# Delta memory: six values at a group's end, mixing quarters built by halves, a routing step moved

## The chip, the cores and the metric

The kernel runs on one core of one Trainium2 chip. Its engines are TensorE (PE; PEld is its weight load), VectorE (DVE), ScalarE (ACT), GpSimd (POOL) and SyncE (SP). The metric is the device time of one execution in microseconds, the median of several runs.

## The reference, cut to what matters

The whole is linear attention, a mixture-of-experts layer (top 2 of 8 experts), a fast-weight ("delta") memory with layer norm, and the expert layer again, each added to x. The change lies in the delta memory and its seam with the second routing. The memory works on 512 batches of 8 steps, 16 heads of 64 values:

```
k = k / sum(k); q = q / sum(q)            # k, q are elu(.) + 1
denom_acc = cumsum(k); key_denom = <shifted denom_acc, k>   # 1 at the first step
beta = sigmoid(beta) * key_denom; k = k / (key_denom + EPS)
for t in range(8):                        # per batch and head, W starts at 0
    delta = beta_t * (v_t - W k_t)
    W = W + outer(delta, k_t)
    out_t = W q_t
layer_out = SCALE * out / (<denom_acc, q> + EPS)
x = x + layer_norm(h + layer_out @ w_o.T) # then the router of the second expert layer
```

## The kernel before, in words

`delta_memory` splits the 512 batches into four groups of 128 (NG = 4), each of 1024 tokens. The kernel never keeps W: for each group it computes all products of keys with keys and queries within a batch ("gram"), solves an 8-step triangular system per batch and head for mixing coefficients, and multiplies the values by these. The stages of group g, or of m = g - 1 where the work is one group behind:

- *Values.* `values(m)` on TensorE (L1839 is `project_value`) makes 16 tiles of 128x512, each of four instructions in the stream (two passes, each with its weight load). ScalarE copies each to `v` (L2023). For m < 3 only the first 12 are made here (LATE_VALUES), with `turn(m + 1)`, the transposes of the next group's h (L1834), ahead of value 8.
- *Keys and queries of g.* For each of eight head pairs TensorE makes four projections (L1897) into a ring of four PSUM banks, ScalarE takes an exponent (L2060), VectorE combines the two into `kq` (L2327) and frees the bank. Then TensorE makes the pair's 128 small products (L1919), and ScalarE copies the two banks out (`gram_copy`, L2049 and L2052). VectorE puts the steps of the former group's solve between its tiles (BESIDE). Values 14 and 15 of m come before the last pair's products, 12 and 13 after them.
- *Store, load, solve.* The products go to DRAM by eight DMAs each from SyncE and GpSimd and come back by one (`load_coef`, L1638). `solve(m, i)`, i = 0 to 16, is a chain of small VectorE instructions from L2176 (betas), L2182 (`key_sums`, which waits for the load) to L2242 (`scale_out`). SyncE then stores and loads the coefficients again (L1646, L1654) as `mix_tok`.
- *Mixing of m.* For each pair p TensorE multiplies values by a spread form of the coefficients (L1967, 64 matmuls in two halves of a bank pair), ScalarE copies the result (L2094), and one pair later TensorE projects it out (`project_out`, L1950). The spread form is made in quarters of the heads: 0 and 1 by VectorE (`build`, L2253), 2 and 3 by ScalarE (its own `build`, L2082, eight instructions of one step each), after the pairs p = 1 and p = 3, needed at p = 4 and p = 6.

The order on each engine is written out by hand, in one function body per engine; each engine runs its instructions in that order and waits for counting semaphores.

Between these stages lie the steps of the second expert layer's router, in eight rounds r of 512 tokens. A round is: normalise (VectorE), `turn` (TensorE transposes, L241), copy (ScalarE, L262), `score` (L247), `choose` (VectorE, from L187), `rank` (TensorE, L254) and the exponent (ScalarE, L266), `place` (VectorE: `weigh` from L210 and `placed` up to L233), then `send`, eight indirect DMAs from GpSimd (L277). All rounds share one PSUM bank, `b_r`. The semaphore `place_ready` is raised once by `begin` and once by each `place`; `turn` waits for it:

```
    def turn(self, pe, r):
        pe.wait_ge(self.place_ready, r + 1)
```

In `mix_values(m)` for m = 1 and 2 TensorE does round 2m - 2 at p = 0, 1, 2 (turn, score, rank) and turn and score of round 2m - 1 at p = 5 and 6; its rank comes in the next `values`. VectorE's steps between the groups are the list of calls near L2440.

## Time and profile before

| | us |
|---|---|
| median of 3 runs | 982.95 (982.76 to 984.05) |
| the profiled execution's own time | 982.38 |
| its span, first to last instruction | 980.7 |
| TensorE busy | 926.1 |
| VectorE busy | 553.3 |
| ScalarE busy | 541.6 |
| GpSimd busy | 370.3 |

The profile is of one execution. Its rows give times from the span's start, so a position such as 562.6 can be found in the timeline of every engine. Matmuls overlap, and a stretch of matmuls ends somewhat before the sum of start and duration says; the distance between two starts is the safer measure. "Idle before" is how long an engine stood before a row, and the name behind the arrow is the instruction that seems to have released it; "issue" means that the profile shows nothing it waited for.

### The profile page before, as it was taken

The numbers are of one execution on the slowest core, as the hardware profiler recorded it, in microseconds if no ns is written. First come the engines' busy times: TensorE is split into PE (matmuls) and PEld (weight loads), VectorE is DVE, ScalarE is ACT, GpSimd is POOL, SyncE is SP. The second block draws the span as 40 slices with busy tenths as digits, with TensorE's granted clock in tenths as the row PEclk, the third lists the DMA queues.
The fourth block names the chain that finished last, engine by engine and source line by source line (L and its number), as shares of the span: only waits on it lengthen the run. The fifth ranks groups of instructions, "written<-read, shape, count | busy, mean of one in ns | idle before, by whom it ended". The sixth has DMA issues, their size and how long they took to land.

```text
span 980.7 us, 31631 instructions
## 1 busy us (share of the span) xinstructions
PE 926.1 (94%) x11919; PEld 689.4 (70%) x11919; DVE 553.3 (56%) x1966; ACT 541.6 (55%) x1082; POOL 370.3 (38%) x387
## 2 busy tenths in 40 slices
PE   7999999999999999987999899999998999989994
PEld 6446655665679999984554485568456779988994
DVE  5236465355376542206679658777885887774114
ACT  3543243334314555544776675785677585666772
POOL 2300412321333776653141012122531264866773
PEclk9999999999999999998999999999999999999998
DMA  8744224404403233205020120111024513123346
GB/s 220 231 89 88 63 53 105 108 15 97 110 23 75 78 97 99 69 24 173 3 88 4 46 89 1 47 49 53 24 58 135 171 48 77 59 72 99 94 123 220
DMA packets 80308, 82.77 MB, mean 84 GB/s; under 512 B 12207, under 2 KB 63236, under 8 KB 79648
## 3 DMA queue, kind: packets, MB, share of 16 engines
q1 hardware_dynamic: 66240, 59.61, 23.0%
q0 software_dynamic: 10176, 19.04, 6.1%
q10 hardware_dynamic: 3744, 2.10, 0.9%
q8 instruction: 99, 1.62, 0.7%
q14 instruction: 49, 0.40, 0.1%
HBM read 53.96 MB, written 27.64 MB: 83 GB/s over the span
## 4 chain that ended last, share of the span: by engine, by line
PE 38%; DVE 8%; ACT 4%; issue 3%; DMA 1%; POOL 0%; DVEq 0%; ACTq 0%; POOLq 0%; SPq 0%
PE b_ring L1897 8%; PE b_ring L1348 6%; PE b_ring L1359 6%; PE b_ring L1839 5%; PE b_g L1950 4%; PE b_g L1919 4%; PE b_ring L1967 2%; ACT early L2082 2%; DVE b_kq L2327 2%; ACT b_outT L2094 1%; DVE b_coef L2238 1%; PE b_r L247 1%; PE b_s L1906 1%; DVE b_prod L2235 0%; PE b_g L1339 0%
## 5 line engine op out<-in xcount | busy, mean ns | idle before, releaser
L1897 PE MATMUL b_ring<-b_hT,b_qkT 128*128 128x512 f32 x256 | 120.9, 609 | 5.9 <-DVE b_kq L2327 4.6
L2327 DVE SCALAR_TENSOR_TENSOR b_kq<-b_exp,b_ring 128x512 f32<-128x512 f32 x128 | 83.0, 684 | 32.1 <-ACT b_exp L2060 30.4
L277 POOL DMA_INDIRECT expert_rows<-f_route_sent,f_route_place_id x64 | 62.4, 976 | 97.5 <-DVE f_route_place_id L233 50.9
L2060 ACT ACTIVATE b_exp<-b_ring 128x512 f32<-128x512 f32 x128 | 73.6, 604 | 30.5 <-PE b_ring L1897 18.0
L1897 PEld LDWEIGHTS b_ring<-b_hT,b_qkT 128*128 128x128 f32 x256 | 45.1, 189 | 62.4 <-issue 39.8
L1021 ACT ACTIVATE phik<-a_ring 128x512 f32<-128x512 f32 x64 | 38.2, 597 | 81.4 <-PE a_ring L864 81.4
L277 POOL DMA_INDIRECT expert_rows<-g_route_sent,g_route_place_id x48 | 53.2, 1108 | 76.8 <-PE b_ring L1967 31.1
L1348 PE MATMUL b_ring<-b_v,b_kq 128*128 128x128 f32 x568 | 76.1, 278 | 3.1 <-issue 2.8
L1359 PE MATMUL b_ring<-wide,b_v 128*128 x568 | 75.9, 277 | 0.6 <-ACT b_v L1389 0.4
L1348 PE MATMUL a_ring<-phik 128*128 128x128 f32 x568 | 75.0, 275 | 0.4 <-ACT phik L1369 0.4
L1359 PE MATMUL a_wide<-wide,phiqT 128*128 x568 | 74.7, 275 | 0.0
L1321 POOL DMA_INDIRECT expert_parts<-phiqT,a_rn_wide x59 | 59.2, 1004 | 39.7 <-ACT phiqT L1389 14.9
L1348 PEld LDWEIGHTS b_ring<-b_v,b_kq 128*128 128x128 f32 x568 | 70.1, 194 | 3.7 <-issue 3.2
L1359 PEld LDWEIGHTS b_ring<-wide,b_v 128*128 128x128 f32 x568 | 69.8, 194 | 1.0 <-issue 1.0
L1348 PEld LDWEIGHTS a_ring<-phik 128*128 128x128 f32 x568 | 69.1, 192 | 0.7 <-issue 0.7
L1359 PEld LDWEIGHTS a_wide<-wide,phiqT 128*128 128x128 f32 x568 | 69.0, 192 | 0.0
L1950 PE MATMUL b_g<-b_oT,b_outT 128*128 128x128 f32 x512 | 64.9, 281 | 4.0 <-ACT b_outT L2094 3.9
L1383 DVE COPY phik<-wide 128x512 f32 x71 | 30.6, 437 | 66.8 <-PE a_ring L1348 59.8
L1321 POOL DMA_INDIRECT expert_parts<-b_v,b_hT x56 | 57.0, 1018 | 23.1 <-PE b_ring L1348 10.9
L1950 PEld LDWEIGHTS b_g<-b_oT,b_outT 128*128 128x128 f32 x512 | 59.4, 191 | 6.4 <-ACT b_outT L2094 4.1
L864 PE MATMUL a_ring<-feat_k,a_xnT 128*128 128x512 f32 x128 | 60.8, 610 | 0.8 <-ACT a_xnT L1015 0.8
L1374 ACT ACTIVATE phiqT<-a_ring 128x512 f32<-128x512 f32 x71 | 42.4, 597 | 34.5 <-PE a_ring L1348 34.5
(340 smaller groups left out, 1845.3 us busy)
## 6 DMA issues: line engine op xcount, KB each, us to landing
a_rn_wide<-norm_compact SPq DMA_DIRECT2D x28, 512.0 KB, 8.4
wide<-in_L_ffn_W SPq DMA_DIRECT2D x32, 256.0 KB, 5.2
a_rn_wide<-expert_rows SPq DMA_DIRECT2D x71, 65.0 KB
b_coef<-gram_compact SPq DMA_DIRECT2D x4, 1024.0 KB, 5.0
b_hT<-expert_rows SPq DMA_DIRECT2D x56, 65.0 KB
x<-in_L_attn_a_x SPq DMA_DIRECT2D x8, 256.0 KB, 4.5
early<-expert_parts SPq DMA_DIRECT2D x4, 512.0 KB, 5.7
gram_compact<-wide SPq DMA_DIRECT2D x32, 64.0 KB
```

The costliest lines, as they stand in the source:

```text
L277: pool.indirect_dma_start(self.rows, bass.IndirectOffsetOnAxis(self.place_id[:, k, n:n + 1], 0), self.sent[:, n, k, :], None).then_inc(sel ...
L864: ins = pe.matmul(bank[:, :], xnT[par][:, n * P:(n + 1) * P], A["feat_k"][:, half * 512:half * 512 + 512], start=True, stop=True)
L1321: pool.indirect_dma_start(self.parts, bass.IndirectOffsetOnAxis(self.blk[u][:, DIM + 1:ROW].bitcast(U32), 0), self.y[u], None, bounds_chec ...
L1348: ins = pe.matmul(self.hid_bank[j % 2][:, f * P:(f + 1) * P], self.w1_now[:, b % W1_SLOTS, f * P:(f + 1) * P], self.blkT[:, b % HID_SLOTS, ...
L1359: ins = pe.matmul(self.y_bank[j % 2][:, 0:P], self.hidT[:, b % HID_SLOTS, f, :], self.C["w2"][:, bass.ds(e, 1), f, :].rearrange("p a c -> ...
L1374: act.activation(self.hidT[:, b % HID_SLOTS, :, :], self.hid_bank[j % 2][:, :].rearrange("p (f n) -> p f n", f=FC), ACT.Relu).then_inc(sel ...
L1839: pe.matmul(value_bank(k)[:, :], hT[:, m % 2, (k // 2) * P:(k // 2 + 1) * P], C["b_vT"][:, (k % 2) * 512:(k % 2) * 512 + 512], start=True, ...
L1897: pe.matmul(ring[n % 4][:, :], w, hT[:, g % 2, half * 512:half * 512 + 512], start=True, stop=True)\
L1919: ins = pe.matmul(g_bank[hh][32 * j:32 * j + 32, a * 64:(a + 1) * 64], kq[r, p % 2, 4 * a + j, 0:T * FOUR], kq[r, p % 2, 4 * a + j, KEYS + ...
L1950: ins = pe.matmul(g_bank[t // 4][:, (t % 4) * P:(t % 4 + 1) * P], outT[:, p % 2, t, :, :], C["b_oT"][:, p, :], start=(p == 0 and t % 4 == ...
L2060: act.activation(exps[:, n % EXPS, :], ring[n % 4][:, :], ACT.Exp, bias=-1.0).then_inc(S["exp_ready"], 1)
L2327: dve.scalar_tensor_tensor(out=kq[:, p % 2, half:half + FOURS // 2, slot:slot + T * FOUR], in0=exps[:, n % EXPS, :].rearrange("p (a n) -> ...
```

## The change

It has five parts. For m = 0 to 2 six values come late instead of four: 14 and 15 before the last pair's products as before, 12 and 13 in the middle of them, 10 and 11 after them. The PSUM banks of the mixing are turned by two, and each wait is set to the new order. ScalarE's quarters are built in two halves of four instructions, after the pairs 1, 2, 3 and 4 instead of whole ones after 1 and 3. In VectorE's list before the last mixing `build(3, 1)` comes directly behind `build(3, 0)`, ahead of `place(3)`. And `place(2)` comes behind the whole of `solve(3, ...)` instead of before it. The arithmetic is the same.

```diff
--- before.py
+++ after.py
@@ -1584,8 +1584,10 @@
 
             return late_res if m == 2 else res
 
-        LATE_VALUES, FIRST_VALUES = 12, 2
-        BESIDE_VALUES, AFTER_VALUES = (14, 15), (12, 13)
+        LATE_VALUES, FIRST_VALUES = 10, 2
+        BESIDE_VALUES, WITHIN_VALUES, AFTER_VALUES = (14, 15), (12, 13), (10, 11)
+
+        LAST_BLOCK = AFTER_VALUES[0] // 2
 
         def values_beside(g):
 
@@ -1593,7 +1595,7 @@
 
         def nth_value(m, k):
 
-            return k if m == NG - 1 or k < LATE_VALUES else (BESIDE_VALUES + AFTER_VALUES).index(k) + LATE_VALUES
+            return k if m == NG - 1 or k < LATE_VALUES else (BESIDE_VALUES + WITHIN_VALUES + AFTER_VALUES).index(k) + LATE_VALUES
 
         def values_between(m):
 
@@ -1890,8 +1892,8 @@
                         n = 4 * p + k
                         if n >= 4:
                             pe.wait_ge(S["kq_ready"], 32 * g + n - 3)
-                        elif g > 0 and n < 2:
-                            pe.wait_ge(S["v_ready"], 16 * (g - 1) + LATE_VALUES - 1 + n)
+                        elif g > 0 and n >= 2:
+                            pe.wait_ge(S["v_ready"], 16 * (g - 1) + LATE_VALUES - 3 + n)
                         kind, half = k // 2, k % 2
                         w = C["b_qkT"][:, (1 - kind) * HD + p * P:(1 - kind) * HD + (p + 1) * P]
                         pe.matmul(ring[n % 4][:, :], w, hT[:, g % 2, half * 512:half * 512 + 512], start=True, stop=True)\
@@ -1913,6 +1915,10 @@
                         pe.wait_ge(S["att_read"], g - 1)
                     wait_apart(pe, S["kq_ready"], 32 * g + 4 * p + 4, K.passed)
                     for a in range(NTAU):
+                        if g > 0 and p == PAIRS - 1 and a == NTAU // 2:
+                            pe.wait_ge(S["kq_ready"], 32 * g + 32)
+                            for k in WITHIN_VALUES:
+                                project_value(g - 1, k)
                         for j in range(4):
                             for hh in range(2):
                                 r = slice(hh * DH, (hh + 1) * DH)
@@ -1929,7 +1935,7 @@
                         spare_values(g)
                     products(p)
                 if g > 0:
-                    pe.wait_ge(S["kq_ready"], 32 * g + 32)
+                    pe.wait_ge(S["v_ready"], 16 * (g - 1) + LATE_VALUES + len(BESIDE_VALUES))
                     for k in AFTER_VALUES:
                         project_value(g - 1, k)
 
@@ -1957,18 +1963,18 @@
                         pe.wait_ge(S["spread_built" if p < 4 else "late_built"], 2 * m + p // 2 % 2 + 1)
                     if p >= 2:
                         pe.wait_ge(S["outT_ready"], 16 * m + 2 * p - 2)
-                    for a in (*range(NTAU - 2), NTAU - 1, NTAU - 2):
-                        if p == 0 and a == NTAU - 2:
+                    for a in (*range(LAST_BLOCK), *range(NTAU - 1, LAST_BLOCK - 1, -1)):
+                        if p == 0 and a == LAST_BLOCK:
                             pe.wait_ge(S["v_ready"], 16 * (m + 1))
                         for j in range(2):
                             r = slice(j * DH, (j + 1) * DH)
                             for hh in range(2):
                                 hd = (2 * p + hh) * DH
-                                ins = pe.matmul(ring[(2 * p + j) % 4][hh * DH:(hh + 1) * DH, :]
+                                ins = pe.matmul(ring[(2 * p + j + 2) % 4][hh * DH:(hh + 1) * DH, :]
                                                 .rearrange("c (t a b) -> c t a b", t=T, a=NTAU)[:, :, a, :],
                                                 v[r, a, hd:hd + DH], spread[r, p // 2 % 2, (2 * p + hh) % QH, a, :, :],
                                                 start=True, stop=True)
-                            if a == NTAU - 2:
+                            if a == LAST_BLOCK:
                                 ins.then_inc(S["mixed_full"], 1)
                     if p >= 1:
                         project_out(p - 1)
@@ -2064,7 +2070,7 @@
                     act.wait_ge(S["own_step"], 2)
                     act.wait_ge(S["parts_added"], 6)
                 m, beside = values_beside(g)
-                for k in beside:
+                for k in (*beside, *(WITHIN_VALUES if g > 0 else ())):
                     copy_value(m, k)
                 gram_copy(PAIRS - 1)
                 for k in AFTER_VALUES if g > 0 else ():
@@ -2072,16 +2078,17 @@
                 act.wait_ge(S["beta_logit"], g + 1)
                 act.activation(beta[:, 0:T, :], sums[:, 0:T, 0:HEADS], ACT.Exp, scale=-1.0).then_inc(S["beta_exp"], 1)
 
-            def build(m, q):
+            def build(m, q, half):
 
                 n = 4 * m + q
                 act.wait_ge(S["tok_loaded"], 32 * (m + 1))
                 act.wait_ge(S["mixed_full"], 4 * (n - 1))
                 by_head = mix_tok[:, :, :, :].rearrange("p a t h -> p h (a t)")[:, q * QH:(q + 1) * QH, :]
-                for b in range(T):
+                for b in range(half * T // 2, (half + 1) * T // 2):
                     ins = act.activation(spread[:, q % 2, :, :, :, :].rearrange("p h a t b -> p h (a t) b")[:, :, :, b], by_head,
                                          ACT.Copy, scale=own[:, b:b + 1])
-                ins.then_inc(S["late_built"], 1)
+                if half:
+                    ins.then_inc(S["late_built"], 1)
 
             def mix_values(m):
                 for n in range(16):
@@ -2091,9 +2098,9 @@
                         act.wait_ge(S["att_done"], PAIRS * m + p - 1)
                     if n == 0 and 0 < m < NG - 1:
                         act.wait_ge(S["x_ready"], m)
-                    act.copy(outT[:, p % 2, :, j, :], ring[n % 4][:, :].rearrange("c (t b) -> c t b", t=T)).then_inc(S["outT_ready"], 1)
-                    if j == 1 and p in (1, 3):
-                        build(m, 2 + p // 2)
+                    act.copy(outT[:, p % 2, :, j, :], ring[(n + 2) % 4][:, :].rearrange("c (t b) -> c t b", t=T)).then_inc(S["outT_ready"], 1)
+                    if j == 1 and 1 <= p < 5:
+                        build(m, 2 + (p - 1) // 2, (p - 1) % 2)
                     if j == 1 and m == NG - 1:
                         if p in (4, 6):
                             routing(routes_of_mixing(m)[0], (p - 4) // 2)
@@ -2439,15 +2446,15 @@
 
             solve(3, 0)
             choose(2)
-            place(2)
             for i in range(1, SOLVE_PARTS):
                 solve(3, i)
+            place(2)
             choose(3)
             residual(2)
             output_statistics(2)
             build(3, 0)
+            build(3, 1)
             place(3)
-            build(3, 1)
             output_normalize(2)
             for i in range(2):
                 scale_and_add(dve, 2, i)
```

## Rows read from the trace of the kernel before

**Rows 1.** the page's part 1: busy us of each engine (share)

```profile
PE 926.1 (94%) x11919; PEld 689.4 (70%) x11919; DVE 553.3 (56%) x1966; ACT 541.6 (55%) x1082; POOL 370.3 (38%) x387
```

**Rows 2.** TensorE's waits over the span: who for whom, us in total, times, longest

```profile
PE b_g L1919 <- issue: 5.2, 2, 2.7
...
PE b_ring L1897 <- DVE b_kq L2327: 4.6, 8, 1.5
PE b_g L1950 <- ACT b_outT L2094: 3.9, 6, 1.0
```

**Rows 3.** TensorE's timeline, group 1's end: start, us, what, [idle before <-releaser]

```profile
562.62 0.31 PE L1919 MATMUL b_g<-b_kq 64*32 64x64 f32 x1 [2.56 <-issue]
562.86 3.54 PE L1839 MATMUL b_ring<-b_vT,b_hT 128*128 128x512 f32 x4
```

**Rows 4.** the timeline of all engines, group 2's end

```profile
650.32 1.98 PE L1839 MATMUL b_ring<-b_vT,b_hT 128*128 128x512 f32 x4
...
652.24 1.66 PE L1967 MATMUL b_ring<-early,b_v 64*64 64x64 f32 x64
```

**Rows 5.** the timeline of all engines, group 3's end

```profile
742.50 0.43 PE L1919 MATMUL b_g<-b_kq 64*32 64x64 f32 x24 [2.69 <-issue]
...
742.86 3.17 PE L1839 MATMUL b_ring<-b_vT,b_hT 128*128 128x512 f32 x4
```

**Rows 6.** windows: us, busy PE, PEld, DVE, ACT, POOL, granted clock, DMA

```profile
562.50:566.50 4.00, 3.88 (x14) 1.47 (x18) 3.29 (x4) 2.58 (x4) 0.85 (x2) 0.57 0.03 8
...
440.00:450.00 10.00, 4.69 (x22) 4.72 (x23) 4.03 (x13) 2.50 (x5) 2.91 (x2) 0.50 0.66 208
```

**Rows 7.** keys of groups 1 to 3: a window, then TensorE's and VectorE's timelines

```profile
511.00:544.00 33.00, 29.69 (x596) 14.06 (x592) 30.91 (x66) 20.55 (x32) 7.84 (x7) 1.00 0.10 35
...
607.56 1.29 DVE L2327 SCALAR_TENSOR_TENSOR b_kq<-b_exp,b_ring 128x512 f32<-128x512 f32 x2
...
608.30 1.99 PE L1897 MATMUL b_ring<-b_hT,b_qkT 128*128 128x512 f32 x4 [0.42 <-DVE b_kq L2327]
...
695.17 0.69 DVE L2327 SCALAR_TENSOR_TENSOR b_kq<-b_exp,b_ring 128x512 f32<-128x512 f32 x1 [1.08 <-ACT b_exp L2060]
```

**Rows 8.** the timeline of the mixings of m = 0 and m = 1

```profile
569.44 5.17 ACT L2082 ACTIVATE early<-b_mix_tok,b_own 128x256 f32<-128x256 f32 x8
...
575.57 2.05 PE L1950 MATMUL b_g<-b_oT,b_outT 128*128 128x128 f32 x16 [0.64 <-ACT b_outT L2094]
...
670.04 2.05 PE L1950 MATMUL b_g<-b_oT,b_outT 128*128 128x128 f32 x16 [1.01 <-ACT b_outT L2094]
```

**Rows 9.** timelines of all engines: load of coefficients, place, solve, turn

```profile
572.97 0.34 SPq L1638 DMA_DIRECT2D b_coef<-gram_compact  x1
...
578.05 0.25 DVE L2182 RECIPROCAL b_rsum<-b_coef 128x16 f32<-128x16 f32 x1 [9.36 <-DMA b_coef<-gram_compact]
...
752.58 0.33 SPq L1638 DMA_DIRECT2D b_coef<-gram_compact  x1
...
756.43 0.17 DVE L210 TENSOR_SCALAR g_route_denom<-g_route_ratio 128x4 f32<-128x4 f32 x1 [1.94 <-ACT g_route_ratio L266]
...
759.12 0.17 DVE L233 CAST g_route_place_id<-g_route_place_of 128x8 uint32<-128x8 f32 x1
...
759.20 0.25 DVE L2182 RECIPROCAL b_rsum<-b_coef 128x16 f32<-128x16 f32 x1
...
765.47 0.47 PEld L241 LDWEIGHTS b_r<-ident,g_route_sent 128*128 128x128 f32 x4
...
776.28 1.22 DVE L2242 SCALAR_TENSOR_TENSOR b_mix<-b_mix,b_rden 128x1024 f32<-128x1024 f32 x1
```

**Rows 10.** the timeline of the last mixing

```profile
789.45 2.10 PE L1967 MATMUL b_ring<-early,b_v 64*64 64x64 f32 x128 [0.36 <-ACT b_v L2023]
...
792.25 2.29 DVE L2253 TENSOR_TENSOR early<-b_mix_tok,b_own 128x2048 f32<-128x2048 f32 x1
...
794.60 1.16 PE L1967 MATMUL b_ring<-early,b_v 64*64 64x64 f32 x64 [0.73 <-DVE early L2253]
```

## The prediction

> **What bounds the kernel now.** I read the page's busy times first: TensorE is busy for 94% of the span, no other engine for more than 56% [rows 1]. So a change pays only where it takes idle time out of TensorE, and costs what idle time it puts in. Next I read the list of waits for TensorE alone [rows 2]. Three kinds stand out, all in the memory part: 5.2 us in two stops within the head products (L1919), put down to "issue"; 3.9 us in six waits of the output projection (L1950) for ScalarE's copies; 4.6 us in eight waits of the key projections (L1897) for VectorE. Then I read the timeline around each group's end, since all edits lie there.
>
> At the end of group 1 TensorE stops for 2.56 us one matmul short of the end, then the two late values take 3.54 us [rows 3]. Group 3 does the same: 2.69 us, then 3.17 us [rows 5]. Group 2 has no stop, and its two values take 1.98 us [rows 4]. The granted clock over 562.5 to 566.5 is 0.57 [rows 6]: the stop also drops the clock to 1.2 GHz for a while. That such a stop is TensorE running out of fetched instructions is my reading, not shown.
>
> **The change, part by part.** Working time is the profiled run's: 982.38 us, span 980.7; the median of three is 982.95, 0.57 more.
>
> *Values.* Per group m = 0 to 2 values 10 and 11 leave the stage before the keys and come after the last products; 12 and 13 come amid these. Nothing is added on TensorE: four passes take 1.9 us wherever they stand (650.32 to 652.24 in [rows 4]). What matters is who limits the stretch they leave. In group 1's keys, VectorE is busy 30.9 of 33 us [rows 7], and TensorE waits for it up to 543 us: the 1.9 us freed before become a longer wait, gain 0. In group 2 VectorE reaches its first key at 607.56 and TensorE waits again at 608.30 [rows 7]: gain 0. In group 3 VectorE idled 1.08 us before its first key [rows 7]: gain 1.1 of the 1.9. The bounds are 0 and 1.9 each; I take these.
>
> At the other end the two values amid the products cost 1.9 us before the products finish. In groups 1 and 3 they run while TensorE would otherwise stop, if the fetch comes as late after it was asked for as before: products finish at 562.9 and with no net cost. Bounds: the whole stop moves elsewhere (+1.9) to both vanish (-0.8). Group 2 has no stop to fill: +1.9. The values after the products in group 1 then run at 2.4 GHz: 3.54 - 1.98 = -1.6. The first mixing pair must end with the block that needs them; ScalarE copies the products first, so the first 64 mixing matmuls take 0.5 more, as in group 2 today (1.66 for 1.16) [rows 4]: -1.1 in group 1.
>
> By the Trainium skill (TensorE: Matmul & The Clock Gate, "HAM oscillation — how this bites in real kernels") time spent throttled costs half of itself. The trace agrees: 3.54 for 1.98. The same section warns only of idle gaps longer than either stop here, by which the values behind them would run at full clock; the rows show otherwise, and they decide.
>
> *Quarters by halves.* ScalarE builds eight parts of a quarter in 5.17 us at a stretch, and TensorE waits 0.64 after each in m = 0 and 1.01 once in m = 1 and in m = 2 [rows 8]. In halves ScalarE spends 2.6 + 1.1 (two copies) per pair against TensorE's 3.1 (1.1 mixing, 2.0 projection): it falls back 0.6 per pair over four pairs but starts a pair ahead, and by my count each copy is just in time. Gain 1.2 in m = 0, 1.0 in m = 1 (bounds 0 and all of it). The new order of PSUM banks only follows the values; the waits keep their distance. 0.
>
> *Builds of the last group together.* VectorE's second build today starts at 792.25, after place(3), and TensorE waits 0.73 for it [rows 10]. Both at once: -0.7; place(3) comes 2.3 later but its consumers (GpSimd's sends) have their own pace. Bounds -0.7 and +0.5 (a later root on GpSimd).
>
> *place(2) behind the whole of solve(3).* This is the edit that decides. It frees VectorE to start solve(3) when its coefficients land: asked for at 752.58, and 5.1 us later by the same load in m = 0 (572.97 to 578.05), so at 757.7 instead of 759.20 [rows 9]. That is worth at most 1.5 us on the way to the last mixing, where TensorE's values end just beside the build: I take 0.4. But place(2) ends with the increment of place_ready, and Router.turn (L238) waits on TensorE for place_ready >= r + 1. For r = 3 that is 4: one from begin, one each from place(0), place(1), place(2). The turn of route 3 stands in mix_values(2) at p = 5, at 765.47 [rows 9], and the diff leaves it there. Behind it in TensorE's queue are the rest of that mixing, all 16 values of the last group and its mixing. So TensorE will stand at that turn until place(2) is done.
>
> When is that? solve(3) takes 759.20 to 777.50 (776.28 + 1.22), 18.3 us of back-to-back VectorE work; place takes from 756.43 to 759.29, 2.9 [rows 9]. Start 757.7 + 18.3 + 2.9 + 0.1 = 779.0, against 765.5: +13.5, if nothing before moved. Bounds of this term: +13.4 with the page's median of 5.0 us to land, +15.0 if the coefficients land only at 759.2.
>
> This time hangs on the end of group 3's products (store, load, solve), so gains up to there count and gains between there and the turn do not. Up to there: -1.1 (group 1), -1.2 (m = 0 halves), +1.9 (group 2), -1.0 (m = 1 halves), -1.1 (keys 3), 0 (group 3, 1.9 against its stop) = -2.5. The turn comes at 776.5, +11.0. The gains of m = 2 (full clock for its values, its halves) only make TensorE arrive earlier, near 761, and wait some 15 us.
>
> After a stop the clock falls: +1.6, the excess of the values behind a stop of 2.56 [rows 3]. From 440 to 450 it stood at 0.50 throughout [rows 6], with TensorE busy for under half of that; half of these 10 us bounds it at +5. From the turn TensorE has the same 24.0 us of work to the last mixing (765.47 to 789.45 [rows 9, 10]), less 0.4 where it waited for VectorE. In the last mixing -0.7, and -0.2, the rest of L1950's 3.9 us. VectorE, GpSimd and the expert stage follow TensorE as today, since they too wait for its values and mixings.
>
> Sum: +11.0 + 1.6 - 0.4 - 0.9 = +11.3, so 993.7 on the profiled run's scale and 994.0 with half of the 0.57 to the median.
>
> **Rivals.**
> (1) Stall as told, but the gains ahead of it don't come: fetch stops move with the matmuls, and halves let ScalarE fall behind. For: the stops depend on positions in the instruction stream, which this shifts by eight. Against: the waits for copies are plainly the 5 us builds. +13.5 + 1.6 + 0 = 997.5. A longer low clock gives the same size.
> (2) The stall is short: TensorE's turn isn't held by place(2), or solve(3) is far shorter with VectorE undisturbed. Then the gains decide: -2.5, another 1.2 at the clock and 1.0 from the halves of m = 2, 0.9 in the last mixing: 982.4 - 5.6 = 976.8, faster. It decides once place(2) is done before about 761. Against: the count of the semaphore is in the code, and the solve's steps depend on each other; I find no way.
> (3) The change of order costs about what the rest gains: a stop of 5 to 6 us, 982 to 983. It would need two thirds of the solve gone.
>
> **How the numbers follow.** Forecast 0.83, rival 1 0.11, rival 2 0.04, rival 3 0.02. The forecast's terms run from 990 (all gains at their best bound) to about 996.5 (clock low for longer); with rival 1, 8 in 10 lie in 990 to 998. A measurement of this kernel tells 0.2% (2 us) from no change: faster 0.04, same 0.02, slower 0.94.
>
> **What would show it.** In the profile after: TensorE's L241 in the third mixing waiting 13 to 17 us for VectorE's place_id (L233), with nothing on TensorE meanwhile, and the granted clock at half behind it; VectorE's L2182 of m = 3 released by the DMA; no L1950 wait for b_outT above 0.3 us; stops in the last products of groups 1 and 3 under 1 us, and L1839 behind them at 2.0, not 3.5 us. TensorE's waits for b_kq in groups 1 and 2 grow by up to 1.9 us each. Wrong would be a third mixing that runs through, or one where another wait than the turn holds TensorE.

## The result, and the profile after

The changed kernel is slower: median 999.71 us of five runs (998.80 to 1000.33), beside 982.76 us for the kernel before in five runs (979.66 to 984.05). The ratio is 1.0185, 95% interval 1.0169 to 1.0200. Forecast were 994.0 us and a range of 990 to 998, so the sign and the mechanism came out and the size did not: the measured median lies 1.7 us above the range. The profiled execution took 998.8 us, span 997.1, where before it took 982.38 us, span 980.7.

Line numbers moved by 2 to 7: head products L1919 are now L1925, keys L1897 are L1899, output projection L1950 is L1956, values L1839 are L1841, mixing L1967 is L1973, the solve's first line L2182 is L2189, GpSimd's shift L1724 is L1726.

The page's part 1 (busy us by engine) of the kernel after:

```profile
PE 929.6 (93%) x11919; PEld 692.2 (69%) x11919; DVE 555.1 (56%) x1966; ACT 540.7 (54%) x1082; POOL 368.4 (37%) x387
```

Counts are those of [rows 1]: the work is the same, and TensorE's share fell because the span grew. The list of waits for TensorE alone says why. Here it is for the kernel after (who for whom, us in total, times, longest):

```profile
PE b_r L241 <- DVE g_route_place_id L233: 17.4, 1, 17.4
PE b_ring L1899 <- DVE b_kq L2334: 9.1, 9, 2.2
...
PE b_g L1925 <- issue: 1.2, 3, 0.6
...
PE b_g L1956 <- ACT b_outT L2101: 0.6, 2, 0.3
```

Against [rows 2]: one new wait of 17.4 us; the waits for VectorE in the keys went from 4.6 to 9.1; the two long stops (5.2) and the waits for ScalarE's copies (3.9) are nearly gone. All four movements were named in the forecast; the first two are larger than it had them.

The new wait, in the timeline of all engines of the kernel after: the coefficients' load, what VectorE does with them, and the turn on TensorE.

```profile
752.57 0.33 SPq L1640 DMA_DIRECT2D b_coef<-gram_compact  x1
...
759.58 0.25 DVE L2189 RECIPROCAL b_rsum<-b_coef 128x16 f32<-128x16 f32 x1 [6.41 <-DMA b_coef<-gram_compact]
...
776.65 1.23 DVE L2249 SCALAR_TENSOR_TENSOR b_mix<-b_mix,b_rden 128x1024 f32<-128x1024 f32 x1
...
780.47 0.17 DVE L233 CAST g_route_place_id<-g_route_place_of 128x8 uint32<-128x8 f32 x1
...
780.70 1.12 PE L241 MATMUL b_r<-ident,g_route_sent 128*128 128x128 f32 x4 [17.36 <-DVE g_route_place_id L233]
```

Compare [rows 9]. VectorE now stands idle for 6.41 us until the coefficients land. Before, place(2) (2.9 us) lay in that gap and cost nearly nothing: the coefficients landed 6.4 us after 752.58, at 759.0, and the solve began at 759.20. Now it lies behind 18.3 us of solve, and TensorE, which has finished its third mixing as far as the turn, waits for it.

What that does to the clock, in windows (us, busy PE, PEld, DVE, ACT, POOL, granted clock, DMA) of the kernel after:

```profile
562.50:566.50 4.00, 4.00 (x125) 2.37 (x124) 2.71 (x4) 3.36 (x6) 0.10 (x1) 1.00 0.02 4
...
768.50:780.50 12.00, 0.00 (x0) 0.00 (x0) 10.79 (x39) 0.00 (x0) 0.00 (x0) 0.51 0.17 51
780.50:785.70 5.20, 5.00 (x77) 4.56 (x78) 0.14 (x1) 1.66 (x3) 2.07 (x2) 0.50 0.58 146
785.70:790.00 4.30, 4.30 (x94) 4.21 (x93) 1.92 (x18) 1.07 (x2) 0.00 (x0) 1.00 0.28 65
```

The first window was at 0.57 before [rows 6] and is at full clock now: the stop at group 1's end is gone. But the long stop puts TensorE at 1.2 GHz (0.51), and it stays there (0.50) for 5 us after it has resumed.

**Where the 16.4 us came from.** I cut both profiled executions at the same instructions (start of the first turn-transpose of the memory part, start of each group's last head product, start of solve(3), of the turn of route 3, of the last mixing, of the expert stage) and compare the stretches. The last column splits the forecast's sum in the same way:

```
us                              before   after   diff   forecast
up to the memory part            452.9   453.6   +0.7    0
group 0, to its last product      47.8    48.4   +0.6    0
groups 1 to 3, to last product   242.0   240.7   -1.3   -2.5
last product to solve(3)          16.5    16.9   +0.4   -1.5
solve(3) to turn of route 3        6.4    21.1  +14.7  +14.9
turn to last mixing               23.8    26.2   +2.4   +1.2
last mixing to expert stage       28.3    27.0   -1.3   -0.9
expert stage to end              162.9   163.1   +0.2    0
sum                                             +16.4  +11.2
```

### The profile page after: what moved, and what is told of

It is laid out like the page before. It is cut to its first block, busy times and chain, and to the rows that moved or that the text cites. A ratio compares the mean times of both kernels' runs of the same rounds, so it can differ in the third digit from the quotient of the medians.

```text
span 997.1 us, 31639 instructions
## 1 busy us (share of the span) xinstructions
PE 929.6 (93%) x11919; PEld 692.2 (69%) x11919; DVE 555.1 (56%) x1966; ACT 540.7 (54%) x1082; POOL 368.4 (37%) x387
## 4 chain that ended last, share of the span: by engine, by line
PE 35%; DVE 14%; issue 2%; DMA 1%; ACT 1%; SPq 0%; DVEq 0%; POOL 0%; ACTq 0%; POOLq 0%
PE b_ring L1899 7%; PE b_ring L1348 6%; PE b_g L1956 5%; PE b_ring L1359 5%; PE b_g L1925 4%; PE b_ring L1841 3%; PE b_ring L1973 3%; DVE b_kq L2334 2%; DVE b_coef L2245 1%; DVE b_h L111 1%; DVE b_prod L2242 1%; DVE b_outT L111 1%; DMA b_coef<-gram_compact 1%; DVE b_ln_stats L90 0%; PE b_s L1908 0%
## 5 line engine op out<-in xcount | busy, mean ns | idle before, releaser
L1899 PE MATMUL b_ring<-b_hT,b_qkT 128*128 128x512 f32 x256 | 122.7, 617 | 10.3 <-DVE b_kq L2334 9.1
L1899 PEld LDWEIGHTS b_ring<-b_hT,b_qkT 128*128 128x128 f32 x256 | 45.7, 191 | 68.2 <-issue 39.8
L1956 PE MATMUL b_g<-b_oT,b_outT 128*128 128x128 f32 x512 | 65.7, 283 | 0.6 <-ACT b_outT L2101 0.6
L1956 PEld LDWEIGHTS b_g<-b_oT,b_outT 128*128 128x128 f32 x512 | 60.3, 194 | 2.7 <-issue 0.8
```

Of the source, the lines that this page charges most:

```text
L1899: pe.matmul(ring[n % 4][:, :], w, hT[:, g % 2, half * 512:half * 512 + 512], start=True, stop=True)\
L1956: ins = pe.matmul(g_bank[t // 4][:, (t % 4) * P:(t % 4 + 1) * P], outT[:, p % 2, t, :, :], C["b_oT"][:, p, :], start=(p == 0 and t % 4 == ...
```

## The experiments

Chips differ. e1 to e4, e6 to e8 and b1 ran on one chip, c0, e5, b2 and b3 on a second, and c1, e9 and e10 on a third. On the first two the stages outside the memory part take some 50 to 65 us longer in every kernel, the one before included (medians of 1037 to 1047 us, against 978.9 on the third). So each kernel is judged by its ratio to the kernel before on the same chip, and a percentage of 1040 is a little more us than one of 980.

### Is it the place? One line each way

Theory: the wait at the turn is the whole loss. Rival: the other edits cost, and the wait only shows where the time is lost.

**e1**, the changed kernel with place(2) back:

```
             choose(2)
+            place(2)
             for i in range(1, SOLVE_PARTS):
                 solve(3, i)
-            place(2)
             choose(3)
```

> The changed kernel with place(2) put back ahead of solve(3, 1); all else stays changed. Theory (TensorE stands at the turn of round 3 until place(2) raises place_ready): L241's wait of 17.4 us goes. TensorE's values of the last group then end near 786.5 on the changed kernel's scale, but the last builds wait for coefficients that go by load (759.6), solve (18.3), store and load (9.4) and one build (2.3), about 789.7 against 806.9 now: 17 us less, so 982 to 983, no gain over the kernel before. Rival (TensorE is held there by something else, such as the late sends or ScalarE's halves): stays above 990. Rival of the prediction (the other edits gain 5.6): 977.

Measured 1.0004 (0.9973 to 1.0034): the loss is gone. The wait for place_id is absent from TensorE's list. A gain of 5.6 us from the other four parts together, as in the prediction's rival 2, would be 0.9946, outside the interval.

**e2**, the kernel before with only place(2) moved behind the solve:

> The kernel before with only place(2) moved behind solve(3). Theory: the whole loss is in this edit. With coefficients landing at about 759.5 the turn comes near 780.5 instead of 765.5, plus about 2.5 for the low clock behind the stop, less 0.4 later: +17, about 999.5. As the prediction had it (landing 5.1 us after issue, low clock worth 1.6): +14.7, about 997.5. Rival (the loss is shared with the other edits): below 993.

Measured 1.0151 (1.0108 to 1.0195): the loss is there without any other edit. From TensorE's list of waits in this kernel:

```profile
PE b_r L241 <- DVE g_route_place_id L233: 14.0, 1, 14.0
```

**e8**, the changed kernel with place(2) amid the solve:

```
             for i in range(1, SOLVE_PARTS):
                 solve(3, i)
+                if i == 5:
+                    place(2)
-            place(2)
```

> The changed kernel with place(2) after solve(3, 5) instead of after the whole solve. Theory: place(2) ends near 759.6 + 8.4 + 2.8 = 770.8 on the changed kernel's scale, so TensorE waits 7.6 us at the turn instead of 17.4, and comes to the last mixing 9.9 us sooner: 989 to 990. The loss is linear in the time of place(2), until it ends before about 763. Rival (it is the sum of VectorE's work, not the place of this step): 999.7.

Measured 1.0087 (1.0059 to 1.0116). Its timeline: the solve's start, the place, the turn.

```profile
784.15 0.25 DVE L2189 RECIPROCAL b_rsum<-b_coef 128x16 f32<-128x16 f32 x1 [5.62 <-DMA b_coef<-gram_compact]
...
795.28 0.17 DVE L233 CAST g_route_place_id<-g_route_place_of 128x8 uint32<-128x8 f32 x1
...
795.50 1.12 PE L241 MATMUL b_r<-ident,g_route_sent 128*128 128x128 f32 x4 [6.80 <-DVE g_route_place_id L233]
```

From the solve's start to the turn it is 11.4 us here, 21.1 behind the whole solve (21.1 in e2, e6, e7, e9 and both profiles of the changed kernel alike) and 4.9 with the place ahead of it (e1). From group 3's last product to the last mixing it is 46.1 us ahead and 53.6 midway; behind it is 61.3 and 61.8 in e7 and e6 on the same chip, and 64.2 and 63.0 in the two traces of the changed kernel. The time follows the position of that one call. One position between the ends was measured, so that the loss is linear is not shown.

### The other edits, one at a time

**e3**, only the values (place, halves and builds as before):

> The kernel before with only the new order of the values and the turned banks. Theory: the gain at the group ends (two stops of 2.6 us filled, full clock behind them) is given back, since group 2 has no stop, groups 1 and 2 wait for VectorE anyway, and in group 3 GpSimd's shift(3) starts 1.7 us sooner and falls on VectorE's output_normalize(1), which takes 5.0 instead of 2.1 us and stops TensorE 2.2 us: 983, within 1.5 of before. Prediction's view (no collision): 980 or less.

Measured 1.0030 (0.9999 to 1.0061): no gain; a loss is not clear of the noise.

**e4**, only the quarters by halves:

```
-            def build(m, q):
+            def build(m, q, half):
...
-                for b in range(T):
+                for b in range(half * T // 2, (half + 1) * T // 2):
...
-                    if j == 1 and p in (1, 3):
-                        build(m, 2 + p // 2)
+                    if j == 1 and 1 <= p < 5:
+                        build(m, 2 + (p - 1) // 2, (p - 1) % 2)
```

> The kernel before with only ScalarE's quarters built by halves. Theory: the waits of L1950 for b_outT (3.9 us) fall to under 1; -3 us if the last mixing's start follows TensorE, -2.3 if it stays with the coefficients' chain: 979.5 to 980.5. Rival (ScalarE falls behind): 983 or more.

Measured 0.9976 (0.9951 to 1.0000), a gain at the edge of what these runs resolve. Its list of TensorE's waits has the copies' wait at the size of the full change:

```profile
PE b_g L1950 <- ACT b_outT L2095: 0.6, 2, 0.3
```

It was 3.8 us in six waits in c0, the kernel before profiled once more (below). But from group 3's last product to the last mixing it takes 46.1 us, only 0.6 less than before (46.7 in both traces): the coefficients' chain (store, load, solve) sets the end there. e4's trace also lacks the stop before group 3's last products (2.69 us before, 2.42 in c0). The stop is missing in e10 and b2 too, which leave the values as they were, so it comes and goes with other edits, and how much of e4's gain is the copies' and how much this stop's isn't separated.

**e5**, only the last group's two builds together:

> The kernel before with only the last group's two builds together. Theory: TensorE's 0.73 us wait for the second build goes, and router waits behind it: -0.7 to -1.3 us, ratio 0.999. Rival (place(3) later delays GpSimd's sends and a root behind them): 1.0005 or more.

Measured 1.0001 (0.9973 to 1.0028), with the kernel before profiled once more beside it (c0, 1047.78 us):

> The kernel before itself, for a trace on the chip of the experiments, where all kernels take some 5% longer. If that is the chip's DMA (the two attention and expert parts), the stretch from the end of group 0's products to the end of group 3's is 242 us as on the first chip and the one from there to the last mixing 46.7, within 1; if the chip is slower altogether, both are longer in proportion.

The stretch from the last mixing to the expert stage is 31.2 us against 32.7 in c0, where the clock was also low for 3.4 us of it. The run as a whole doesn't show it: 1.5 us are 0.14% and below what these runs resolve. As to c0's own question, the stretch from group 0's products to group 3's is 243.5 us (242.0 on the first chip) and from there to the last mixing 46.7 (46.7). The first is half a us beyond the "within 1" that was expected; in proportion to the whole it would be 258. So the extra time of this chip lies outside the memory part.

### What made it 5 us worse than forecast?

Two things in the trace of the changed kernel were not in the sum. First, a GpSimd instruction (shift(3)) ran into VectorE's output_normalize(1), which then took longer. Timeline of all engines of the kernel after, keys of group 3:

```profile
690.69 5.00 DVE L111 TENSOR_SCALAR b_outT<-b_outT,b_ln_out_meanvar,b_ln_out_rstd 128x128 f32<-128x128 f32 x8
...
692.98 2.36 POOL L1726 TENSOR_TENSOR x<-x,ln_b 128x1024 f32<-128x1024 f32 x1
...
696.34 5.40 PE L1899 MATMUL b_ring<-b_hT,b_qkT 128*128 128x512 f32 x8 [2.24 <-DVE b_kq L2334]
```

Before, shift(3) started at 694.71, behind output_normalize(1), and this took 2.14 us:

```profile
691.96 2.14 DVE L111 TENSOR_SCALAR b_outT<-b_outT,b_ln_out_meanvar,b_ln_out_rstd 128x128 f32<-128x128 f32 x8
...
694.71 2.37 POOL L1724 TENSOR_TENSOR x<-x,ln_b 128x1024 f32<-128x1024 f32 x1
```

GpSimd's rows go out once LATE_VALUES values are in, now 10 rather than 12, so all its work behind them starts sooner. Second, the coefficients took 7.0 us to land (752.57 to 759.58), not 5.1. Right behind them SyncE asks for the expert weights, in this kernel as in the one before.

**e6**, the changed kernel, shift(3) held until output_normalize(1) is done:

```
                 pool.wait_ge(S["h_ready"], m + 2)
+                if m in (3,):
+                    wait_apart(pool, S["normed"], m - 1, K.passed)
                 pool.tensor_tensor(x_group(m)
```

> The changed kernel with GpSimd's shift(3) held until output_normalize(1) is done. Theory (the two instructions hold each other up): VectorE's L111 of b_outT near 690 goes from 5.0 back to 2.1 us, TensorE's wait for b_kq there from 2.24 to under 1, the clock doesn't fall at 697, and all later work comes about 3 us sooner: 996.5. Rival (VectorE is late for its own order of work): unchanged, 999.7.

Measured 1.0155 (1.0122 to 1.0187). Its timeline has VectorE back at its old pace, and the shift behind it:

```profile
711.38 2.30 DVE L111 TENSOR_SCALAR b_outT<-b_outT,b_ln_out_meanvar,b_ln_out_rstd 128x128 f32<-128x128 f32 x8
...
713.85 2.36 POOL L1728 TENSOR_TENSOR x<-x,ln_b 128x1024 f32<-128x1024 f32 x1 [0.20 <-issue]
```

So the collision is what stretches VectorE's row. Group 3, from group 2's last product to its own, took 92.6 us against 94.3 and 94.4 in the two kernels on the same chip that kept the collision (e7, e8). The ratio lies between what was expected of the theory (1.014) and of the rival (1.017) and decides nothing.

**e7**, the changed kernel, expert weights asked for only when the last coefficients are in:

```
+            wait_apart(sp, S["coef_loaded"], NG * 16, K.passed)
             load_experts(sp, C, inp, C["w_in"][1])
             store_mix(NG - 1)
```

> The changed kernel with SyncE's loads of the expert weights held until the last coefficients have landed. Theory (the 1 MB of coefficients took 7.0 us instead of 5.1 since the weights' loads share the DMA engines): they land 5.1 us after issue, the turn comes 1.9 us sooner, 997.8. Rival (the load is as slow alone): unchanged, 999.7.

Measured 1.0180 (1.0150 to 1.0210): no gain, as the rival had it.

**b1**, e1 with shift(2) and shift(3) held as in e6:

> The changed kernel with place(2) back and GpSimd's shift(2) and shift(3) each held until the output_normalize beside it is done. Theory: 3 us from shift(3); shift(2) fell on a substitution step of VectorE (2.57 instead of 0.43 us near 603) in both kernels, up to 2 us more, if it does not hold up the next steps instead: 977.5 to 980. Rival (the collision only moves on to the following steps of VectorE): 981 to 983.

Measured 1.0012 (0.9980 to 1.0044): no gain over e1 (1.0004), where 977.5 to 980 us (about 0.995 to 0.997) were expected.

On the third chip the question was whether collision and load together are the missing 5 us. c1 is the changed kernel once more, **e9** is e6 and e7 together:

> The changed kernel itself, beside the experiments. By the parts: place(2) alone 1.015, the rest 1.0004, so 1.0155 to 1.018. If the first measurement's +17 us was partly the chip's, below 1.014.

> The changed kernel with shift(3) held until output_normalize(1) is done and the weights' loads until the last coefficients have landed: both are what the prediction's sum left out. Theory (collision 2.9 and low clock behind it, load 1.9): 4 to 5 us less than the changed kernel, ratio 1.012 to 1.014, which is the prediction's +11.3 and about 1 for a longer low clock. Rival (the miss has another cause, such as the stop's length itself): 1.016 or more.

Measured: c1 1.0174 (1.0145 to 1.0203), e9 1.0168 (1.0137 to 1.0199). The medians differ by 0.8 us, not by four or five. The traces say why. The changed kernel, second profile (c1):

```profile
696.62 1.98 PE L1899 MATMUL b_ring<-b_hT,b_qkT 128*128 128x512 f32 x4 [2.23 <-DVE b_kq L2334]
...
751.97 0.33 SPq L1640 DMA_DIRECT2D b_coef<-gram_compact  x1
...
757.37 0.25 DVE L2189 RECIPROCAL b_rsum<-b_coef 128x16 f32<-128x16 f32 x1 [4.82 <-DMA b_coef<-gram_compact]
...
778.51 1.12 PE L241 MATMUL b_r<-ident,g_route_sent 128*128 128x128 f32 x4 [15.78 <-DVE g_route_place_id L233]
```

and e9:

```profile
698.19 1.98 PE L1902 MATMUL b_ring<-b_hT,b_qkT 128*128 128x512 f32 x4 [1.43 <-DVE b_kq L2337]
...
751.50 0.33 SPq L1640 DMA_DIRECT2D b_coef<-gram_compact  x1
...
756.50 0.25 DVE L2192 RECIPROCAL b_rsum<-b_coef 128x16 f32<-128x16 f32 x1 [4.41 <-DMA b_coef<-gram_compact]
...
777.64 1.12 PE L241 MATMUL b_r<-ident,g_route_sent 128*128 128x128 f32 x4 [15.38 <-DVE g_route_place_id L233]
```

The same program that took 7.0 us for its coefficients in one execution took 5.4 in the next, so most of the 1.9 I had charged to the weights is not a fixed cost. With the weights held it took 5.0 (e9), 4.9 (e7) and 5.3 (b3) from issue to landing. With them right behind it, it took from 5.3 to 7.0 in the other kernels that wait for this load (e6, c1, e8, e2, after), 6.4 in the kernel before, and only 4.8, 4.9 and 5.0 in e3, e1 and b2. The two sets overlap, so no run here shows what the weights cost. And removing the collision leaves TensorE a wait of 1.43 us where it had 2.23: VectorE is the late one in these keys anyway.

**e10**, the kernel before with shift(2) held behind its own output_normalize:

> The kernel before with only shift(2) held until output_normalize(0) is done. Theory: the substitution step near 603 takes 0.43 instead of 2.57 us, TensorE's first waits for b_kq in group 2 shrink by up to 0.8 and group 2's products end up to 1.8 us sooner: ratio 0.998 to 0.999. Rival (TensorE, not VectorE, sets that stretch): 1.000.

Measured 0.9994 (0.9975 to 1.0013), as the rival had it. In the trace the step does take 0.43 us rather than 2.57, and group 2 from group 1's last product to its own takes 86.8 us (87.6 in the kernel before, on another chip), but the median doesn't show it.

### A version that beats both

**b2** is the kernel before with the halves, the two builds together and both shifts held (values and place as before); **b3** also holds the weights.

> The kernel before with the halves, the last builds together, and shift(2) and shift(3) held until the output_normalize beside them is done; values and place(2) as before. Theory: -2.2 from the halves up to group 3's products, -1.8 from shift(2) no longer holding up a substitution step, -0.4 at the last mixing's start (the coefficients' chain sets it), -0.9 in it: -5.3 us, ratio 0.995. Rival (that chain or VectorE takes most of it back): 0.998 or more.

> The same with the expert weights' loads held until the last coefficients have landed. Theory: place(2) ends about when these land, so at most 1 us more: ratio 0.994 to 0.995. Rival (weights come too late for the expert stage, or the load was not slowed): 0.996 or more.

Measured: b2 0.9953 (0.9929 to 0.9977), faster than both kernels; b3 0.9986 (0.9965 to 1.0008), not the 0.994 to 0.995 expected. Nothing in these runs says why b3 loses what b2 gains; their intervals overlap, so it may be no difference at all, and their profiled executions go the other way (1038.8 us for b3, 1042.9 for b2). e4's halves alone had 0.9976; which of b2's other parts adds to that isn't separated, and b2's trace, like e4's, lacks the stop in group 3.

## Why the prediction was wrong in size and right in kind

The stall, which decides, came as told. Three terms beside it were mis-sized, and they are the step that failed: the gains ahead of it (-2.5 forecast, -1.3 measured, the miss all in group 3), the coefficients' load (5.1 us forecast, 7.0 measured) and what follows the stop (+1.2 forecast, +2.4 measured).

**The stall (right).** The step that decides was sized at 18.3 + 2.9 + 0.1 = 21.3 us from the coefficients' landing to the turn. It measured 21.1 (759.58 to 780.70), and the same in each of six traces (after, c1, e2, e6, e7, e9). e1 and e2 show that this one call makes the loss, e8 that the loss is smaller with less of the solve ahead of it.

**The gains ahead of it (mis-sized).** The forecast took -2.5 us up to the last products of group 3. The profile shows -1.3 in groups 1 to 3, and against it +0.6 in group 0 and +0.7 before the memory part, so the products end at 742.7 as before. The 0.7 is not the change's: in c1 the memory part starts at 452.7. The 0.6 is a stop of 0.56 us in group 0's products, put down to "issue":

```profile
487.48 0.51 PE L1925 MATMUL b_g<-b_kq 64*32 64x64 f32 x34 [0.56 <-issue]
```

It goes with the execution and not with the change: e2, whose group 0 is that of the kernel before, has it (group 0 takes 48.2 us), and e6, whose group 0 is that of the changed kernel, has not (47.2).

From one group's last product to the next one's the forecast had 0, -0.4 and -2.1 us for groups 1, 2 and 3; measured were -0.5, -0.8 and 0.0. So all of the miss is in group 3. Within the -2.5, the failed term is the keys'. For the values that left the stretch ahead of the keys I took 0, 0 and -1.1 us. TensorE's waits for b_kq in the kernel after, one for each group:

```profile
515.42 3.70 PE L1899 MATMUL b_ring<-b_hT,b_qkT 128*128 128x512 f32 x8 [1.08 <-DVE b_kq L2334]
...
606.25 1.98 PE L1899 MATMUL b_ring<-b_hT,b_qkT 128*128 128x512 f32 x4 [2.12 <-DVE b_kq L2334]
```

with the 2.24 at 696.34 shown above; before there was none in group 1 at this place, 0.42 in group 2 and none in group 3. They grew by 1.1, 1.7 and 2.2: of the 1.9 us freed, most came back as a wait in group 2 and more than all in group 3. For groups 1 and 2 that is what the forecast said. For group 3 I took the 1.08 us in which VectorE idled before its first key for slack that could be used; the 2.9 us that the collision added to output_normalize(1) used it up, so the term is +0.3 rather than -1.1 (2.2 of wait for 1.9 freed). The slack would not have given 1.1 without the collision either: there the wait is still 1.43 (e6, e9), which leaves 0.5 of the 1.9 (an estimate). The low clock of 3.4 us behind that wait comes on top in this execution: group 3 took 92.5 us with it and 91.6 in c1, the same program without it. I had asked what the earlier values set free for TensorE and VectorE, not for GpSimd, whose gate the same constant moves. e3 agrees that the values as a whole gain nothing.

**Values amid the products (right).** Group 1's end in the kernel after:

```profile
562.66 1.03 PE L1925 MATMUL b_g<-b_kq 64*32 64x64 f32 x64
563.62 1.98 PE L1841 MATMUL b_ring<-b_vT,b_hT 128*128 128x512 f32 x4
```

No stop, and 1.98 us rather than 3.54 [rows 3]; group 3 is alike (742.87, 1.98 for 3.17 in [rows 5]). The stops put down to "issue" fell from 5.2 to 1.2 us in total. For group 1 all runs agree: the eight traces with the old order of values stop for 2.0 to 2.6 us there, the nine with the new one for 0.5 at most. For group 3 the edit isn't the only way out: three of the eight with the old order (e4, e10, b2) have no such stop either. Why the stops arise wasn't tested.

**Halves (right).** 3.9 to 0.6 us of waits, by the change and by e4 alone. ScalarE's timeline in the kernel after shows a half of 2.7 us between two pairs of copies, in place of 5.17 at a stretch [rows 8]:

```profile
568.91 2.68 ACT L2088 ACTIVATE early<-b_mix_tok,b_own 128x256 f32<-128x256 f32 x4
571.44 1.08 ACT L2101 COPY b_outT<-b_ring 128x512 f32<-128x512 f32 x2
572.38 2.64 ACT L2088 ACTIVATE early<-b_mix_tok,b_own 128x256 f32<-128x256 f32 x4
```

**The solve's start (mis-sized: -1.5 forecast, +0.4 measured).** I took 5.1 us for the load from the same load of m = 0. It was 7.0 here and 5.4 in c1. The load of the last group itself had taken longer than 5.1 in the kernel before; the DMA issues between 750 and 762 us of its trace give KB and us to landing:

```profile
b_coef<-gram_compact SPq DMA_DIRECT2D x1, 1024.0 KB, 6.4
```

So moving place(2) away could bring the solve only 0.2 us forward, not 1.5, and 1.3 of the 1.9 us missed here could be read before the change; the other 0.6 is the spread between executions. The bound I gave (759.2) was close to what came.

**Behind the stop (mis-sized: +1.2 forecast, +2.4 measured).** Turn to last mixing took 26.2 us; the forecast had 23.8 + 1.6 - 0.4 = 25.0. The excess behind the stop was taken from a stop of 2.56 us, and this one was 17.4. The low level outlasted the stop by 5.0 us here, 5.8 in c1 and 3.6 in e9, at half speed: 2.5, 2.9 and 1.8 us. The bound in the prediction (10 us low, +5) held it; the value taken came from the wrong row. The -0.4 was a misreading: [rows 10] puts that wait down to ScalarE's copy of the values (b_v L2023), not to VectorE, and as much is there in the kernel after:

```profile
806.86 2.10 PE L1973 MATMUL b_ring<-early,b_v 64*64 64x64 f32 x128 [0.36 <-issue]
```

**Last mixing (-0.9 forecast, -1.3 measured).** There is no wait for the second build any more. In e5 alone that stretch was 1.5 us shorter than in c0, part of which may be c0's low clock.

The miss between the two profiled executions is thus +0.7 start, +0.6 group 0, +1.2 gains ahead, +1.9 load, -0.2 stall, +1.2 behind the stop (0.9 clock, 0.4 the wait that stayed, -0.1 rest), -0.4 last mixing, +0.2 expert stage: 5.2. Between the medians it is 5.7. Settled as a repeatable cost are the clock and, in kind, the missing gain of the keys. The start, group 0's stop and most of the load's 1.9 go with the execution (in c1 the load is 0.3 over the forecast). With c1's load the sum would stand near 997, inside the range but well above the forecast: the range was too narrow above a forecast whose gains all had to arrive on the same path. What stays open is why the load's time spreads so, and why the medians of e9 and the changed kernel differ by less than their traces' stretches do.

**Rivals.** Rival 1 (stall as told, gains ahead don't come, 997.5) came nearest, at a chance of 0.11. I gave it too little because I argued against its causes (fetch, ScalarE late). Neither of these is what happened (the long stops are gone, and the copies' wait is 0.6); the gains failed by VectorE's lateness in group 3's keys instead. The longer low clock, which the rival names in passing, did come. Rivals 2 and 3 are out by the stop of 17.4 us.

## What to carry to other kernels

Before moving a small step that others wait for behind a long one, look at what the engine did at the old place: here VectorE idled for its coefficients there, so the step was nearly free, and behind the solve it cost 15 us of TensorE. Take a transfer's time from the same transfer in the trace, not from a sister of it: the last load took 6.4 us where the second took 5.1. When a threshold is lowered, list every engine that waits on it; an engine released sooner can land on another's work. And a gain upstream of a new bound is worth something only if it reaches the chain that sets it, so give such gains a chance to be nought together.

## What the runs showed of the hardware

- A VectorE row of eight TENSOR_SCALAR of 128x128 takes 2.14 us alone, and 5.00, 4.99 and 4.74 when GpSimd's 2.36 us TENSOR_TENSOR of 128x1024 starts in it (after, c1, e3): VectorE lost 2.6 to 2.9 us, a little more than the whole of GpSimd's instruction, while that one kept its 2.36. Apart the row takes 2.14 to 2.30 (before, e6, e9). A single TENSOR_TENSOR of 128x256 on VectorE took 2.57 us when it began 0.07 us behind the same GpSimd instruction (before), and 0.43 with that instruction held (e10):

```profile
602.84 2.35 POOL L1724 TENSOR_TENSOR x<-x,ln_b 128x1024 f32<-128x1024 f32 x1
602.91 2.57 DVE L2238 TENSOR_TENSOR b_coef<-b_coef,b_prod 128x256 f32<-128x256 f32 x1
```

  By the Trainium skill (SBUF — State Buffer, "SBUF: two separate sides") GpSimd shares a pair of ports with a VectorE instruction that has two SBUF inputs or runs in a two-port mode, and whoever starts first holds the pair for its whole instruction while the other stands. The rows agree with it: the TENSOR_TENSOR ends 0.29 us after GpSimd's (605.48 and 605.19). No run here tells ports from another cause, nor in which mode the eight TENSOR_SCALAR ran.
- A stop of 2.1 to 2.2 us may or may not bring the clock down. Windows over the keys of groups 2 and 3 (columns as above), the kernel after:

```profile
605.00:612.00 7.00, 5.38 (x144) 2.79 (x144) 6.79 (x17) 2.98 (x5) 0.46 (x1) 1.00 0.00 0
692.00:702.00 10.00, 7.76 (x37) 2.86 (x43) 9.72 (x18) 3.97 (x8) 5.08 (x5) 0.83 0.06 20
```

  and c1, the same program:

```profile
605.00:612.00 7.00, 6.42 (x104) 2.86 (x107) 6.72 (x16) 2.99 (x5) 0.46 (x1) 0.76 0.00 0
692.00:702.00 10.00, 7.43 (x94) 3.09 (x95) 9.76 (x19) 4.46 (x8) 5.15 (x5) 1.00 0.05 18
```

  After, the clock falls to 1.2 GHz behind the stop of 2.24 us (0.83 of 10 us is 3.4 us at half) and not behind that of 2.12; in c1 it falls behind the one of 2.12 and not behind that of 2.23. By the Trainium skill (TensorE: Matmul & The Clock Gate, "HAM oscillation — how this bites in real kernels") only longer idle gaps bite; these rows and [rows 6] show that such short ones can. Over all seventeen traces, 14 of the 29 stops of 1.9 to 2.7 us in the memory part came with the low clock. What it cost in these keys, where VectorE is late too, is 1.0 us each: between the two executions group 2 took 86.7 and 87.7 us, group 3 92.5 and 91.6, the longer each time the one with the low clock.
- After a stop of 14.0 to 17.4 us at the turn the low clock lasts 3.3 to 5.8 us past the resumption (six traces: after, c1, e2, e6, e7, e9), though TensorE is busy for 5.0 of the first 5.2 us in the kernel after.
- The same 1 MB reload of the last group's coefficients took 4.8 to 7.0 us from issue to landing in the fourteen executions with the weights' loads right behind it, and 4.9, 5.0 and 5.3 in the three with them held; it took 5.4 and 7.0 in two executions of one program. The reloads of the groups ahead, with no weights behind, took 4.7 to 5.7 us, and once 6.5 (e3).
